# Second attention: one VectorE signal for each pair of score matmuls, in place of one for each matmul

## What is computed

```
def _L1_attn_ref(x, Wqkv, Wout, Wpos, coeffs):
    ...
    pos_bias = jnp.einsum('ijf,hf->hij', pos_feat, Wpos)
    qkv = jnp.einsum('bsd,ed->bse', x, Wqkv)
    q, k, v = jnp.split(qkv, 3, axis=-1)
    ...
    logits = jnp.einsum('bihd,bjhd->bhij', q, k) * scale + pos_bias[None]
    attn = jax.nn.softmax(logits, axis=-1)
    out = jnp.einsum('bhij,bjhd->bihd', attn, v).reshape(B, S, D)
    return jnp.einsum('bsd,ed->bse', out, Wout)

x = _layernorm(x + _L0_attn_ref(x, ...), axis=-1)
x = _layernorm(x + _L0_ffn_ref(x, ...), axis=-1)
x = _layernorm(x + _L1_attn_ref(x, ...), axis=-1)
x = _layernorm(x + _L1_ffn_ref(x, ...), axis=-1)
```

## Time and profile before

| | |
|---|---|
| three runs | 2300.39 us median (2293.86 to 2314.51) |
| the profiled execution | 2308.74 us, of which the profile's span is 2306.9 us |
| TensorE matmuls busy | 1875.7 us (81%) |
| VectorE busy | 1487.1 us (64%) |
| ScalarE busy | 1078.0 us (47%) |
| GpSimd busy | 804.0 us (35%) |
| mean granted TensorE clock | 0.919 of full |
| second attention | from 801.1 to about 1998 us |

### The profile page before, as it was taken

How to read it: one execution, slowest core, us unless ns; L and a number is a source line. 1 busy time by engine, 2 the same in 40 slices (tenths; PEclk the granted TensorE clock), 3 DMA queues, 4 the chain that set the end, 5 groups by cost and what they waited for, 6 DMA issues and landing times. The chain is left out here.

```text
span 2306.9 us, 49879 instructions
## 1 busy us (share of the span) xinstructions
PE 1875.7 (81%) x15436; PEld 958.0 (42%) x15436; DVE 1487.1 (64%) x4594; ACT 1078.0 (47%) x2723; POOL 804.0 (35%) x811
## 2 busy tenths in 40 slices
PE   8487878787478489888888888888888998669896
PEld 6255655555456223333323333233233333346554
DVE  6268788887421377677667767677577777333277
ACT  3355555555134145555545555555455555423221
POOL 4458788887410302212221222212221220100166
PEclk9789899999789689999999999999999999879998
DMA  3453322332078223334233323332333232134333
GB/s 110 156 183 108 105 100 72 108 107 98 30 215 252 82 77 107 113 93 111 71 103 93 110 73 108 95 106 71 106 96 107 71 109 82 60 126 160 132 97 98
DMA packets 147129, 248.05 MB, mean 108 GB/s; under 512 B 20628, under 2 KB 49316, under 8 KB 146356
## 3 DMA queue, kind: packets, MB, share of 16 engines
q1 hardware_dynamic: 137828, 220.80, 31.8%
q0 software_dynamic: 9072, 24.41, 3.9%
HBM read 198.16 MB, written 121.96 MB: 139 GB/s over the span
## 5 line engine op out<-in xcount | busy, mean ns | idle before, releaser
L1793 DVE CUSTOM_DVE_ANT_0 c_sums<-c_s,bias 128x512 f32<-128x512 f32 x1024 | 663.6, 686 | 277.5 <-PE c_s L1431 223.4
L1640 ACT ACTIVATE c_pT<-c_u 128x512 f32<-128x512 f32 x1024 | 572.2, 597 | 544.8 <-PE c_u L1449 462.4
L1449 PE MATMUL c_u<-spread_line,c_pick 128*32 128x512 bf16 x4096 | 326.8, 397 | 40.4 <-DMA spread_line<-tops_d 40.4
L1463 PE MATMUL c_o<-c_pT,c_vst 128*32 128x256 f32 x4096 | 325.6, 394 | 12.6 <-ACT c_pT L1640 8.6
L1431 PE MATMUL c_s<-c_kst,c_qst 64*128 64x512 bf16 x1024 | 245.9, 408 | 42.4 <-DVE c_tops L1793 23.4
L1439 PE MATMUL c_u<-c_qst,c_kst 64*128 64x512 bf16 x1024 | 230.1, 393 | 25.0 <-issue 15.8
L523 ACT ACTIVATE v<-a_bank,gain 128x64 f32<-128x64 f32 x768 | 165.8, 343 | 58.0 <-DVE vp L737 58.0
L1463 PEld LDWEIGHTS c_o<-c_pT,c_vst 128*32 128x32 f32 x4096 | 123.0, 113 | 138.6 <-issue 27.5
L1387 POOL DMA_INDIRECT zs_d<-c_xs,c_slot x64 | 63.2, 988 | 310.1 <-DMA zs_d<-in_zeros 260.6
L389 PE MATMUL a_bank<-wv,xT 128*128 128x512 f32 x256 | 155.4, 695 | 18.3 <-ACT v L523 14.0
L1449 PEld LDWEIGHTS c_u<-spread_line,c_pick 128*32 128x32 bf16 x4096 | 62.3, 95 | 245.5 <-issue 193.7
(11 more groups left out here) (263 smaller groups left out, 2898.9 us busy)
## 6 DMA issues: line engine op xcount, KB each, us to landing
xs_d<-in_zeros SPq DMA_DIRECT2D x16, 2048.0 KB
zs_d<-in_zeros SPq DMA_DIRECT2D x16, 2048.0 KB
spread_line<-tops_d SPq DMA_DIRECT2D x256, 64.0 KB
parts_d<-c_parts SPq DMA_DIRECT2D x32, 384.0 KB
c_kst<-parts_d SPq DMA_DIRECT2D x256, 48.0 KB
c_qst<-parts_d SPq DMA_DIRECT2D x256, 48.0 KB
d_w<-in_wd SPq DMA_DIRECT2D x24, 384.0 KB
b_w<-in_wb SPq DMA_DIRECT2D x24, 321.0 KB
```

The lines of the kernel that those rows point to most:

```text
L1449: mm = nc.tensor.matmul(u_ps[bank_of(n)][ARRAY * k:ARRAY * (k + 1), :].rearrange("k (t q) -> k t q", t=T), pick[:, c, k, :], line[:, G * j ...
L1463: mm = nc.tensor.matmul(o_ps[ARRAY * i:ARRAY * (i + 1), half * 2 * P:(half + 1) * 2 * P], vst[s.par][:, c, f:f + ARRAY], pT[r % 2][:, i, h ...
L1640: nc.scalar.activation(pT[n // G % 2][:, n % G, :], u_ps[bank_of(n)][:], ACT.Exp).then_inc(sem("exp_done"), 1)
L1793: v.tensor_tensor_reduce(sums[n % 2][:], s_ps[bank_of(n)][:], bias, 1.0, -3.0e38, ALU.add, ALU.max, top_s[j % 2][:, k:k + 1]).then_inc(sem ...
```

## The change

TensorE adds to `s_ps` only with the second matmul of each pair, and VectorE waits on it only ahead of the pair's first top, for as many pairs as it needs (SLOTS = 32 pairs a batch). The matmuls, tops, their order, banks and the other waits stay.

```
@@ -1428,8 +1428,10 @@
                     h = G * j + i
-                    nc.tensor.matmul(s_ps[bank_of(n)][:], qst[rows_of(h), h // 2, t * P:(t + 1) * P], kst[rows_of(h), h // 2, :],
-                                     start=True, stop=True).then_inc(sem("s_ps"), 1)
+                    mm = nc.tensor.matmul(s_ps[bank_of(n)][:], qst[rows_of(h), h // 2, t * P:(t + 1) * P], kst[rows_of(h), h // 2, :],
+                                          start=True, stop=True)
+                    if n % 2 == 1:
+                        mm.then_inc(sem("s_ps"), 1)
@@ -1785,7 +1787,8 @@
                     if n % TILES == 0:
                         need(dve, sem("m_ps"), group_of(s, j) - 1)
-                    dve.wait_ge(sem("s_ps"), ALL * s.b + n + 1)
+                    if n % 2 == 0:
+                        dve.wait_ge(sem("s_ps"), SLOTS * s.b + n // 2 + 1)
                     need(dve, sem("top_ready"), ALL * s.b + n - 1)
```

## The result

The changed kernel takes 2318.94 us in the median of eight runs (2308.73 to 2327.24), the kernel before 2305.3 us in eight (2293.86 to 2314.51). The ratio is 1.006, with a 95% interval of 1.0031 to 1.0088: 14 us slower, 7 to 20 by the interval. The forecast was 2311 us, in a range of 2292 to 2328, worked out from the first three runs of the kernel before (median 2300.39); on the median of eight its 10.5 us would give 2316.

The account below looks back on a forecast made before the run. TensorE and VectorE were taken to wait for each other in the second attention, neither full. Bank rule 4.2 us plus register operations 6.3 made 10.5, on the median 2300.4 giving 2311 us; range 2292 to 2328.

Parts of the forecast that it names:

- the first of the ways told: The main forecast, chance 0.58: slower by 10.5 us, from later tops at batch boundaries and register operations in the loop.
- Nothing is gained over the kernel before by the removed signals and waits: At each pair's second top: its wait was already hidden behind the first top's 0.61 us, so removal wins nothing.
- The bank rule at the boundary: Top of 62 must wait for matmul 63, 0.23 us late; with the smaller case 0.28 a batch, 4.2 us in all.
- The smaller case at pair 5: Pair at 1383.86: second matmul released about 0.05 us after the first, so its top is 0.05 late and TensorE waits.
- The price of a register operation: Behind the score wait of each pair's first top in loop batches: 0.09 us, bounds 0 to 0.12.
- The seven places: Tops per loop batch where the register operation's delay reaches TensorE: 7 x 0.09 = 0.63 us, 6.3 us over 10 batches.
- The places at 1396.85 and 1404.71: Two of the seven: VectorE idle 0.82 and 1.39 us for a score, TensorE waiting later; 0.09 us counted at each.
- The other stages: Sign of being right: stages outside the second attention keep their 1110 us, while that one grows to about 1207.
- Hidden: Rival, chance 0.20: TensorE's other waits, on ScalarE or DMA, end later than the tops; result 2300, within 3 us.
- Slower by more: Rival, chance 0.17: VectorE's turn between pairs becomes the bound, up to 0.32 us at one in three waits: 27 us, 2328.
- the mark that I had set: Sign of being wrong: TensorE's 258 score load waits, 123.2 us, grow by more than 15 us.
- Faster: Rival, chance 0.05: VectorE's "remote" waits are late TensorE signals, and fewer signals halve them; 20 us won, 2280.

Follow-up runs that it names:

- e2: Kernel before with one wait for both matmuls ahead of each pair's first top, each matmul still signalling: 2314.76 us, ratio 1.007.
- e3: Kernel before, with one wait for both matmuls only at the first and last pair of each batch: 2302.41 us, ratio 1.001.
- e1: Changed kernel with a top's two waits swapped, score wait last: ratio 1.0065 on the first chip, 1.0042 when repeated on the third.
- the control, e9: Kernel before, unchanged, run once more on the third chip: 2233.57 us, ratio 1.0026.
- e4: Kernel before with each score signal counting two, so a register operation follows each top's score wait in the loop; no pair wait: 2324.61 us, ratio 1.0114.
- e10: Changed kernel, unchanged, run once more on the third chip: 2242.98 us, ratio 1.0064 to the kernel before.
- e6: Kernel before with the odd step in the turn of the three banks moved from score 63 to 51, second chip: 2231.98 us, ratio 0.9994.
- e8: Kernel before with the two waits of each top swapped, score wait last, on the second chip: 2230.94 us, ratio 0.9984.

## Why the prediction held, point by point

**The whole.** 10.5 us forecast, 14 us measured (7 to 20), and 9 to 14 on the third chip. It was the first of the ways told, and both of its mechanisms are in the rows. That the sum came so near is partly luck: its terms for the register operation were too large, two of its seven places don't bear their term, and the waits that can be read make 7 us.

**Nothing is gained over the kernel before by the removed signals and waits: right.** The second top still follows the first by 1377.72 - 1377.10 = 0.62 us, and e2, with all signals, can't be told from the changed kernel by its time.

**The bank rule at the boundary: right, and its size too.** Forecast: the top of 62 starts 0.60 after matmul 63, 0.23 late, and TensorE's score 1 as late. e3 does this part alone: 0.60, and 0.24 later. With the register operation on top the change shows 0.66 and 0.30, in the loop, forecast 0.32. 15 boundaries give 3.6 us, and e3's time (+4.0) fits, though its interval is wide. e1, which has no register operation behind the wait, is 7.1 us above the control on the third chip; that holds the bank rule, the pair wait at all pairs, and the register operation's cost at pairs 3 and 30. The smaller case at pair 5 (0.05) isn't there in peeled batches: pair 3's second matmul isn't held (0.003 us behind its first), and pair 5's wait grows by 0.01 only. In the loop the register's share comes with it.

**The price of a register operation: the term was too large.** I took 0.09 us from two VectorE instructions that wait in different ways. At the tops it is 0.663 - 0.605 = 0.058 us (e4), and 0.672 - 0.613 = 0.059 in the changed kernel, where the pair wait itself adds 0.008. So the whole lag of an ordinary first top in the loop is 0.067 us, not 0.09. The sequencer's records say what the term left out. A register operation does take 87 ns until the next instruction starts, near the 0.09. But with it the score wait leaves the semaphore instruction ahead of the top, and that one shrinks from 50 ns with two waits to 21 ns with one: 87 - 29 = 58. In peeled batches the lag is 0.008, as forecast ("stays").

**The seven places: five could be read, in four pairs, and all five bear.** Pair 0 is the boundary (0.297 in the loop, forecast 0.32). At pairs 3, 5 and 30 TensorE's wait grew by 0.057, 0.194 and 0.055 us. The pairs 3 and 5 are those of the chain 1383.16, 1384.47, 1386.65, for which the forecast had 0.09 + 0.14 + 0.09; pair 30 is the one of 1371.94, for which it had 0.09. The two of 0.06 are the operation's 58 ns, though not in the way that the term was priced: e1 has them too, with no register operation behind the score wait. Here is the chain in the changed kernel's timeline:

```profile
1385.65 0.50 PE L1431 MATMUL c_s<-c_kst,c_qst 64*128 64x512 bf16 x2
...
1386.43 0.69 DVE L1796 CUSTOM_DVE_ANT_0 c_sums<-c_s,bias 128x512 f32<-128x512 f32 x1
...
1388.72 0.69 DVE L1796 CUSTOM_DVE_ANT_0 c_sums<-c_s,bias 128x512 f32<-128x512 f32 x1 [0.17 <-issue]
...
1389.00 0.86 PE L1431 MATMUL c_s<-c_kst,c_qst 64*128 64x512 bf16 x2
...
1389.47 0.09 PEld L1431 LDWEIGHTS c_s<-c_kst,c_qst 64*128 64x128 bf16 x1 [0.38 <-DVE c_tops L1796]
```

Pair 3's second matmul starts 0.11 us behind its first (0.50 - 0.39), pair 5's 0.47 behind (0.86 - 0.39), and its load had waited 0.38 where it was 0.16: a lag that is handed from pair to pair on a busy VectorE adds up, as the working said. Its top at 1388.72 shows 0.17 us of idle time put down to "issue", time in which nothing in the profile holds it: the table of waits has 17.8 us in 42 of them (on the third chip 13.8 us in 34, and 9 in the control).

**The places at 1396.85 and 1404.71: the step that failed.** I read there long idle times of VectorE (0.82 and 1.39 us) and TensorE waits of 0.50 and 1.24 us behind them, and counted 0.09 us each. In the changed kernel the pair of the first waits 0.4 us less, that of the second 0.45 us more, and neither is the change's doing: at these pairs signals of TensorE arrive 2 to 3 us late on this chip. On the third chip TensorE doesn't wait at the second at all (0.003 us), so that term doesn't exist there. The wait at the first (pair 11) grows there by 0.19 us in the median, from 0.473 to 0.666, but it swings from batch to batch between 0.003 and 0.59 in the control and between 0.003 and 1.02 in the changed kernel, so nothing could be counted on it either. I had seen the odd wait and asked only whether the change would halve it, not whether it was a place to count on.

**The other stages: wrong as a sign.** "The other stages keep their 1110" was meant to show that the traces can be set against each other. They took 2306.9 - 1203.2 = 1103.7 us. A single execution swings by 7 us in stages that nobody touched, half of the effect looked for. The stage from 1196.9 to 1203.2 instead of 1207 says little for the same reason.

**The rivals.** *Hidden* falls: TensorE's waits for tops grew in each pair of traces, by 16 us on the first chip and 10 on the third. *Slower by more* falls in its size: loads waited 267 times instead of 258 and 16 us longer, 1 us above the mark that I had set, but on the third chip 10.1 us, and no place other than the seam shows 0.3 us. *Faster* falls: of TensorE's signals that come over 1 us late there were 183 among 2516 before (7.3%) and 159 among 2004 after (7.9%). Fewer signals are not late less often, and "remote" grew instead of shrinking.

**What is left open.** The four readable waits (pairs 0, 3, 5 and 30) grew by 0.60 us a loop batch, 6 us, and the peeled boundaries add 5 x 0.24 = 1.2: 7 us, against 9 to 14 measured on the third chip. The rest isn't spread evenly: between the control and e10 the median slots of 24 of the 32 pairs agree within 0.01 us, and besides the four only pairs 8, 11, 16 and 24 differ (-0.39, +0.21, -0.15 and +0.07 us in the mean). These four swing by as much or more from batch to batch within one kernel, so what the change does there can't be read from single traces, and the missing 2 to 7 us, if they are real, stay open. The register operation's own share can be read in the rows: 0.058 at pair 0, 0.057 at pair 3, 0.055 at pair 30, and at pair 5 at least the 0.087 that e1 gives back, 0.26 us a loop batch or 2.6 us in all, against 6.3 forecast. No run's time shows it by itself: e1 leaves part of it in, and e4 changes TensorE too.

## What to carry to other kernels

A wait that covers two results binds the first consumer to whatever holds back the second producer: before merging waits, look for pairs in which the second matmul itself waits for a buffer, since there the consumer that frees the buffer becomes late and the producer pays (0.24 us at each of 15 boundaries). In a loop with register compares, look at what the compiler makes of a merged count: a new product meant one more sequencer instruction, 58 ns on each pair's first top, while the removed wait had cost nothing that the rows show. When an experiment is to change one thing, count the sequencer's instructions of every engine in its trace, not only of the one that was meant: e4 put 998 on TensorE, and e1 left in place what it was to take away. And a place with an odd wait in one trace is not a term of the sum until another execution, best on another chip, shows it too.

## What the runs showed of the hardware

**Late signals.** On the first chip, in all its kernels, two bursts in each batch (about pairs 11 to 12 and 20 to 22) have TensorE's completion signals reach the other engines mostly 2 to 3 us after the matmul's end. Over 1 us late in the second attention: 183 of 2516 before, 159 of 2004 after, 150 of 2004 in e1, 179 of 2516 in e3. On the second and third chips: 9 of 2516 (e6 and e9 alike), 5 of 2004 (e10). (The first chip's traces also lack some records of signals, 1021 instead of 1040 of the scores' semaphore, and a missing one would be counted as late.) In the trace of before, around the place of the earlier trace rows:

```profile
1401.53 0.98 POOL L1387 DMA_INDIRECT zs_d<-c_xs,c_slot  x1 [0.30 <-issue]
...
1401.82 0.61 PE L1431 MATMUL c_s<-c_kst,c_qst 64*128 64x512 bf16 x2
...
1401.93 0.58 ACT L1640 ACTIVATE c_pT<-c_u 128x512 f32<-128x512 f32 x1
...
1402.82 0.97 POOL L1387 DMA_INDIRECT zs_d<-c_xs,c_slot  x1 [0.30 <-issue]
...
1404.09 0.97 POOL L1387 DMA_INDIRECT zs_d<-c_xs,c_slot  x1 [0.30 <-issue]
...
1406.04 1.09 ACT L1640 ACTIVATE c_pT<-c_u 128x512 f32<-128x512 f32 x2 [3.53 <-DMA ys_d<-b_y]
```

ScalarE stands idle for 3.53 us though the matmuls that it waits for are done, and the top at 1404.71 is that of the pair at 1401.82, 2.89 us after its matmul. The table of waits of before puts this time down to releasers that have nothing to do with it, "remote" for VectorE and a DMA for ScalarE:

```profile
ACT c_pT L1640 <- DMA ys_d<-b_y: 65.5, 22, 4.3
```

Neither row is in the table of the control on the third chip. GpSimd issues its indirect scatters during the first burst, but it issues the same ones on the other two chips, where hardly any signal is late; the cause was not shown. The price is large: a loop batch takes 76.17 us on the first chip and 69.86 on the third, and the whole kernel 2298.41 against 2230.60 us (3%); slot by slot, the pairs 12 to 14 and 21 to 23 are 7.0 us longer in the trace of before than in the control's, and the others 0.7 us shorter together. Over the kernel the 68 us are five times what the change costs; that the late signals make all of them is argued from where the time lies, and not shown by a run.

**What a wait costs on VectorE's sequencer.** In ordinary pairs of the kernel before, the semaphore instruction ahead of a top starts 0.428 us after the matmul, takes 50 ns with its two waits, and the top starts 127 ns after its end: 0.605. In the loop of e8 it carries one wait and takes 21 ns: 0.428 + 0.021 + 0.127 = 0.576. In e4 a register operation has the score wait; it is 40 ns long in its record, but the next instruction starts 87 ns after it, and that one has one wait: 0.428 + 0.087 + 0.021 + 0.127 = 0.663. With 8 ns for the lone second signal that gives 0.671 in the changed kernel (read: 0.672). Where one instruction carries both waits, the late one last instead of first saves 42 ns (peeled batches of e8).

**A signal that counts two.** With an increment of 2 on the score matmul (e4) the wait no longer stands on its weight load, 998 semaphore instructions of 51 ns came in on TensorE, and a matmul that waits for a top starts 0.84 us after that top's start instead of 0.75.
